# Second attention: maxima issued in pairs, work moved off VectorE beside the projections, stack loads moved to SyncE

## The reference

```python
def _L1_attn_ref(x, attn_qkvw, attn_qkvb, attn_ow, attn_ob):
    HEADS = 32
    B, S, H = x.shape                      # 1, 1024, 512
    hd = H // HEADS                        # 16
    scale = 1.0 / np.sqrt(hd)
    qkv = x @ attn_qkvw + attn_qkvb
    qkv = qkv.reshape(B, S, 3, HEADS, hd)
    q, k, v = (jnp.transpose(qkv[:, :, n], (0, 2, 1, 3)) for n in range(3))   # shortened
    scores = jnp.einsum('bhqd,bhkd->bhqk', q, k) * scale
    probs = jax.nn.softmax(scores, axis=-1)
    ctx = jnp.einsum('bhqk,bhkd->bhqd', probs, v)
    ctx = jnp.transpose(ctx, (0, 2, 1, 3)).reshape(B, S, H)
    return ctx @ attn_ow + attn_ob
```

## Time and profile before

| | |
|---|---|
| runs | 1622.28, 1622.95, 1625.58 us |
| the profiled execution, own time | 1626.14 us |
| its span, first to last instruction | 1624.2 us |
| mean granted TensorE clock | 0.961 |
| busy: PE, DVE, ACT, POOL | 1502.8, 1038.6, 810.8, 232.0 us |
| maxima on PE (line 1578), 512 | 187.1 us busy |
| their reductions on DVE (line 1681), 512 | 319.7 us busy |
| scores (line 1595), 256 | 158.1 us busy |
| mix (line 1610), 1024 instructions | 139.0 us busy |

### The profile page before, as it was taken

One profiled execution on the slowest core, in us unless ns is written; L12 is line 12 of the kernel. 1 busy time (PEld: TensorE's weight loads), 2 busy tenths in 40 slices (PEclk: granted clock), 3 DMA queues, 4 the chain that ended last, 5 costly groups with the idle time before them and its releaser, 6 DMA issues. The chain is left out here.

```text
span 1624.2 us, 22378 instructions
## 1 busy us (share of the span) xinstructions
PE 1502.8 (93%) x8030; PEld 991.4 (61%) x8030; DVE 1038.6 (64%) x2048; ACT 810.8 (50%) x1467; POOL 232.0 (14%) x233
## 2 busy tenths in 40 slices
PE   6867999999999999959979999898999999999987
PEld 4645776666777676647868887786553333333264
DVE  5744666666666666644643433564888999999245
ACT  5325666666666666641221221222117777777834
POOL 2762111112111111100000000001000122331200
PEclk9977999999999999989979999998989999999999
DMA  4142221212122221134212110117420222320001
GB/s 137 53 191 72 85 69 63 69 63 69 63 92 76 69 69 40 34 103 162 97 53 77 59 59 20 52 50 186 148 27 14 72 74 76 77 66 15 18 14 46
DMA packets 63298, 116.83 MB, mean 72 GB/s; under 512 B 12830, under 2 KB 32414, under 8 KB 61902
## 3 DMA queue, kind: packets, MB, share of 16 engines
q1 hardware_dynamic: 59956, 106.63, 20.6%
q10 hardware_dynamic: 3168, 8.65, 2.1%
q0 software_dynamic: 64, 0.11, 0.0%
HBM read 83.04 MB, written 29.66 MB: 69 GB/s over the span
## 5 line engine op out<-in xcount | busy, mean ns | idle before, releaser
L1681 DVE TENSOR_REDUCE ah_minus_half<-ah_ring 128x1 f32<-128x512 f32 x512 | 319.7, 679 | 40.3 <-PE ah_ring L1578 40.0
L968 DVE CUSTOM_DVE_ANT_0 mh_score<-mh_score,mh_mask 128x128 f32<-128x128 f32 (+7 forms) x256 | 195.8, 765 | 179.4 <-PE mh_score L781 179.3
L1641 ACT ACTIVATE ah_probs<-ah_score 128x1024 f32<-128x1024 f32 x256 | 248.7, 1023 | 114.6 <-PE ah_score L1595 113.6
L890 ACT ACTIVATE mh_probs<-mh_score,mh_minus_max 128x128 f32<-128x128 f32 (+7 forms) x256 | 189.6, 741 | 39.8 <-DVE mh_minus_max L968 35.8
L1578 PE MATMUL ah_ring<-ah_k_stack,ah_q_stack 48*128 48x512 f32 x512 | 187.1, 468 | 14.1 <-DVE ah_minus_half L1681 4.2
L1578 PEld LDWEIGHTS ah_ring<-ah_k_stack,ah_q_stack 48*128 48x128 f32 x512 | 82.8, 190 | 176.9 <-DVE ah_minus_half L1681 161.5
L1595 PE MATMUL ah_score<-ah_q_stack,ah_k_stack 49*128 49x512 f32 x512 | 158.1, 445 | 3.8 <-DVE ah_v L1705 2.3
L779 PE MATMUL mh_score<-shared,h_hi 128*128 128x512 f32 (+3 forms) x384 | 152.2, 396 | 3.0 <-ACT mh_probs L890 2.9
L1041 POOL TENSOR_TENSOR h_lo<-mh_pe,h_hi 64x512 fp32r<-64x512 f32 x64 | 81.9, 1279 | 459.0 <-ACT h_hi L876 455.4
L1610 PE MATMUL ah_mix<-ah_probs,ah_v 128*32 128x512 f32 x1024 | 139.0, 615 | 0.6 <-ACT ah_probs L1641 0.6
L781 PE MATMUL mh_score<-shared,h_lo 128*128 128x512 f32 (+3 forms) x384 | 133.0, 346 | 0.0
(11 more groups left out here) (222 smaller groups left out, 2854.7 us busy)
## 6 DMA issues: line engine op xcount, KB each, us to landing
mh_w<-in_w_pairs SPq DMA_DIRECT2D x16, 896.0 KB, 5.6
x<-in_w_inner SPq DMA_DIRECT2D x14, 768.0 KB, 4.1
pe_scratch<-fr_pe_out SPq DMA_DIRECT2D x4, 2048.0 KB, 6.6
mh_pe<-pe_scratch SPq DMA_DIRECT2D x16, 512.0 KB, 4.0
mh_spread<-inverse_scratch SPq DMA_DIRECT2D x64, 128.0 KB, 2.9
a_scratch<-mh_mixed SPq DMA_DIRECT2D x32, 256.0 KB, 2.4
x<-a_scratch SPq DMA_DIRECT2D x8, 1024.0 KB, 6.9
qk_scratch<-ai_ring SPq DMA_DIRECT2D x32, 256.0 KB, 2.7
```

The source lines that it names most:

```text
L890: nc.scalar.activation(probs[:, s % 2, 0:width], score_ps[s % 2][:, base:base + width], ACT.Exp, bias=minus_max[:, s % 4:s % 4 + 1], scale ...
L968: nc.vector.tensor_tensor_reduce(out=scores, in0=scores, in1=mask[:, S - width:S], scale=-1.0, scalar=3e38, op0=ALU.add, op1=ALU.min, accu ...
L1641: nc.scalar.activation(probs[:, 2 * (u % 2) + c, :], score_ps[c][:].rearrange("p e n -> p (e n)"), ACT.Exp, scale=MHA_SCALE).then_inc(prob ...
L1681: nc.vector.reduce_max(minus_half[:, m:m + 1], ring[:, m % 3, :], AX.X, negate=True).then_inc(max_taken, 1)
```

## The change

1. Maxima go in pairs. `two_maxima` waits once, for reduction m-2 (m is the first of the pair), and issues m and m+1, one on each row half.
2. Beside products 8 to 23 there are 6 maxima for each (FIRST = 96), a pair after step 0, a pair after steps 1 and 2, a pair after step 3. The other 416 are spread over the first 116 units, 4 or 2 for each: a pair ahead of c0 and a pair ahead of c1, none ahead of the mix (AHEAD 4 for 6; the inversions keep 6 as INVERTED).
3. DVE keeps only the first four lower parts and weight pieces 0 and 1. From product 4 on ACT evicts each bank twice (once rounded, once whole into a new tile `full`), and POOL subtracts. POOL splits weight pieces 2 to 11. Pieces 6 and 7 come at product 5 instead of 7.
4. ACT copies V without a bias; POOL adds the bias of V after the division.
5. SP holds back the stores of products 4 and later until the stacks of group 0 have landed.
6. The reloads of stacks for groups 3 to 7, one transfer behind each unit's exponentials on ACT before, are issued by SP in one run of twelve.
7. `as_c` and `as_spread` share memory with `full`; the bias comes as one small tensor.

```diff
     def product(self, pe, n, steps):
         if steps[0] == 0:
-            wait(pe, self.lo_ready, min(n - 3, self.NQK))
+            wait(pe, self.first_lo_ready, min(n - 3, 4))
+            wait(pe, self.full_ready, min(n - 7, self.NQK - 4))
             wait(pe, self.v_ready, n - 3 - self.NQK)
...
     def take_upper(self, act, n):
...
+        if n >= 4:
+            wait(act, self.lo_ready, n - 7)
+            self.nc.scalar.activation(self.full[:, n % 4, :], self.bank(n), ACT.Identity, bias=self.bias[:, row:row + 1]
+                                      ).then_inc(self.full_ready, 1)
...
+    def take_lower(self, pool, n):
+        pool.wait_ge(self.hi_ready, n + 1)
+        pool.wait_ge(self.full_ready, n - 3)
+        self.nc.gpsimd.tensor_tensor(self.ring[:, n % 4, 1, :], self.full[:, n % 4, :], self.ring[:, n % 4, 0, :].bitcast(F32),
+                                     ALU.subtract).then_inc(self.lo_ready, 1)
...
     def divide(self, pool, g, half):
...
+        self.nc.gpsimd.tensor_scalar(self.c[rows, cols], self.c[rows, cols], self.bias[rows, 2 * ND + k:2 * ND + k + 1], None, ALU.add
+                                     ).then_inc(self.multiplied, 1)
...
-        FIRST = 5 * (products.COUNT - FROM)
-        AHEAD = 6
+        FIRST = 6 * (products.COUNT - FROM)
+        AHEAD, INVERTED = 4, 6
...
-            return min(FIRST - (-unit * (TOTAL - FIRST) // (UNITS - NT - AHEAD)), TOTAL)
+            return min(FIRST - 2 * (-unit * (TOTAL - FIRST) // (2 * (UNITS - NT - AHEAD))), TOTAL)
...
-            now, then = maxima_at(n), maxima_at(n + 1)
-            return (now, min(now + (then - now + 1) // 2, then), min(now + (3 * (then - now) + 2) // 4, then))[stage]
+            return maxima_at(n) if stage == 0 else min(maxima_at(n) + 2, maxima_at(n + 1))
...
+            def reload_stacks(g, row_halves):
+                wait(sp, scores_ready, 2 * NUNIT * (g - DEPTH + 1))
+                load_stacks(sp, g, row_halves)
...
             load_stacks(sp, 0, (0,))
+            sp.wait_ge(stacks_in[0], 16 * (STACK_DMAS + 2))
             for n in range(4, products.NQK):
...
                 shares.put(sp, g - 1, 1, out, out_taken)
+                if DEPTH <= g + 2 < GROUPS:
+                    reload_stacks(g + 2, range(2))
                 put_max(g, 1)
...
-            def one_maximum(m):
-                wait(pe, max_taken, m - 2)
-                maximum(m).then_inc(max_ready, 1)
+            def two_maxima(m):
+                wait(pe, max_taken, m - 1)
+                for n in range(2):
+                    maximum(m + n).then_inc(max_ready, 1)
...
-                for part in range(2):
-                    products.product(pe, n, range(2 * part, 2 * part + 2))
+                for part, steps in enumerate(((0,), (1, 2), (3,))):
+                    products.product(pe, n, steps)
...
+            for t in range(NT):
+                act.wait_ge(products.ready, products.NQK + t + 1)
+                nc.scalar.copy(v[t][:].rearrange("p (h r) -> p h r", h=H)[:, :, 0:HD],
+                               products.bank(products.NQK + t).rearrange("p (h r) -> p h r", h=H)).then_inc(products.v_ready, 1)
```

More of the change, by code:

```diff
@@ L1313, in take_upper @@
         if n == 0:
[L1314 removed]
+            act.wait_ge(self.bias_in, 16)
         act.wait_ge(self.ready, n + 1)
@@ L1318, in take_upper, with take_first_lower @@
         row = kind * ND + blk
-        self.nc.scalar.activation(self.ring[:, n % 4, 0, :], self.bank(n), ACT.Identity, bias=self.bias_qk[:, row:row + 1]
+        self.nc.scalar.activation(self.ring[:, n % 4, 0, :], self.bank(n), ACT.Identity, bias=self.bias[:, row:row + 1]
                                   ).then_inc(self.hi_ready, 1)
-    def take_lower(self, dve, n):
+        if n >= 4:
+            wait(act, self.lo_ready, n - 7)
+            self.nc.scalar.activation(self.full[:, n % 4, :], self.bank(n), ACT.Identity, bias=self.bias[:, row:row + 1]
+                                      ).then_inc(self.full_ready, 1)
+    def take_first_lower(self, dve, n):
         kind, blk, _ = self.place(n)
@@ L1325, in take_lower @@
         dve.wait_ge(self.hi_ready, n + 1)
-        self.nc.vector.scalar_tensor_tensor(self.ring[:, n % 4, 1, :], self.bank(n), self.bias_qk[:, row:row + 1],
-                                            self.ring[:, n % 4, 0, :].bitcast(F32), ALU.add, ALU.subtract).then_inc(self.lo_ready, 1)
+        self.nc.vector.scalar_tensor_tensor(self.ring[:, n % 4, 1, :], self.bank(n), self.bias[:, row:row + 1],
+                                            self.ring[:, n % 4, 0, :].bitcast(F32), ALU.add, ALU.subtract).then_inc(self.first_lo_ready, 1)
+    def take_lower(self, pool, n):
[3 more added lines that the diff above has]
+                                     ALU.subtract).then_inc(self.lo_ready, 1)
+        pool.wait_ge(self.lo_ready, n - 3)
     def store(self, sp, n, qk):
@@ L1331, in store @@
         first = (kind * ND + blk) * P
-        for part, done in ((0, self.hi_ready), (1, self.lo_ready)):
-            sp.wait_ge(done, n + 1)
+        for part in range(2):
+            if part == 0:
+                sp.wait_ge(self.hi_ready, n + 1)
+            elif n < 4:
+                sp.wait_ge(self.first_lo_ready, n + 1)
+            else:
+                sp.wait_ge(self.lo_ready, n - 3)
             sp.dma_start(qk[part, first:first + P, half * BANK:(half + 1) * BANK],
@@ L1539, in then @@
                 pool.wait_ge(pool_done, n[0])
+            for job in range(products.NQK):
+                if job >= 4:
+                    products.take_lower(pool, job)
+                for i in pieces.get(job, ()):
+                    products.lower(pool, i)
+                    pool.wait_ge(products.w_ready, i + 1)
             for t in range(NT):
@@ L1623, in _ @@
                     while done < maxima_before(n, stage):
-                        one_maximum(done)
-                        done += 1
+                        two_maxima(done)
+                        done += 2
                     if n < UNITS and stage < 2:
@@ L1700, in turn @@
                 last.then_inc(rows_ready, 1)
-            def take_value(n):
-                t = n - products.NQK
-                dve.wait_ge(products.ready, n + 1)
-                nc.vector.tensor_tensor(v[t][:].rearrange("p (h r) -> p h r", h=H)[:, :, 0:HD],
-                                        products.bank(n).rearrange("p (h r) -> p h r", h=H),
-                                        products.bias_v[:].rearrange("p (h r) -> p h r", h=H), ALU.add).then_inc(products.v_ready, 1)
             for half in range(NHALF):
                 nc.vector.memset(minus_max[half][:], 0.0).then_inc(cleared, 1)
-            pieces = {1: (2, 3), 3: (4, 5), 7: (6, 7), 8: (8,), 9: (9,), 10: (10,), 11: (11,)}
             m, joined, turned, inverted = 0, 0, 0, 0
             for n in range(products.COUNT + 1):
-                if n < products.NQK:
-                    products.take_lower(dve, n)
-                elif n < products.COUNT:
-                    take_value(n)
-                for i in pieces.get(n, ()):
-                    products.lower(dve, i)
-                until = maxima_beside(n + 1, 1) if n + 1 < products.COUNT else FIRST if n < products.COUNT else TOTAL
+                if n < 4:
+                    products.take_first_lower(dve, n)
+                until = maxima_beside(n + 1, 2) if n + 1 < products.COUNT else FIRST if n < products.COUNT else TOTAL
                 while m < until:
@@ L1971, in two_layers @@
                 stage = layer.enter_context(ExitStack())
+                offsets["full"] = nc.sbuf_base
+                full = sb("full", [P, 4, BANK])
                 products = Products(nc, layer, stage, io, h, at, d_free)
@@ L1989, in two_layers @@
                          "zeros": at("ah_zeros", [P, D], F32, "down_lo", 6 * S), "scales": at("ah_scales", [P, D], F32, "down_lo", 6 * S + D)}
-                shares = Shares(nc, layer, scratch, h)
+                shares = Shares(nc, layer, scratch, h, products.bias, at, "full")
                 mha_heads(nc, io, scratch, later, shares, products, place)
```

52 lines of the change are left out of this document (20 added, 32 removed).

## The result

The changed kernel takes 1634.16 us, the median of five runs (1633.22 to 1642.62), against 1624.22 for the kernel before beside it (1622.28 to 1626.34). The ratio of the runs is 1.0078, 95% interval 1.0048 to 1.0107: slower by 0.5 to 1.1%. The profiled execution took 1633.22 us, its span is 1631.3 us, 7.1 more than before, and its mean granted clock 0.969 instead of 0.961. It is the shortest of the five runs; by the medians the change costs 9.9 us, by the ratio 12.7.

The account below looks back on a forecast made before the run. Units were taken as bound by a loop of latencies over three PSUM banks, not one engine. Units +10.5, products +5.3, step -6.1 gave +9.7 on the profiled 1626.14 us: 1635.8, less 3.2 for the median, 1632.7 (1622 to 1643).

Parts of the forecast that it names:

- The pair in the units: Second attention's units: long ones 2.94 us instead of 2.70, short 1.89 instead of 2.12, fewer last units; +10.5 us.
- The 4 us for DVE's side work: Units 5 to 115: DVE's turns, joins and inversions add 4 us to the loops instead of 9.7.
- Products: V products: three groups of maxima instead of two make a product 4.67 us instead of 4.39; +5.3 us, ends 0 and +8.
- The first stacks: Stack loads before the first maximum: held stores were not in their way, so the hold costs 0, ends -3 and +3.
- the two signs named: First maximum: still near 1129.6 us as forecast; near 1126 would mean the stores had been in the way.
- Step to the units: Last V product to unit 5: scores start sooner, full clock from 1207 on, 13.9 us instead of 19.95; -6.1 us.
- the 1.3 us for the table load: Step to the units: ACT's load of the exponential's table, hidden before, now stands ahead of the first exponential.
- Off the path: ACT's evictions, POOL's work, SP's reloads and the maxima's shorter lead have room; no term in the sum.
- DVE as the pace: Rival, faster: pairs relieve PE and DVE sets the units' pace; 1580 us, 4%.
- hidden changes of tile: Rival, faster: tile changes hide beside the V products, about 3.8 us each; 1619.5 us, 6%.
- a hardly longer unit: Rival: c1 streams beside the second pair, long units 2.83 us instead of 2.94; 1623 us, no change, 9%.
- The slow clock in the first units: Rival, slower: four long units at about 4.8 us, step term +1 instead of -6.1; 1640 us, 17%.

Follow-up runs that it names:

- Experiment 4: Kernel before with only the units' maxima in pairs ahead of c0 and c1, 80 maxima beside the products as before: 1650.11 us, ratio 1.0159.
- experiment 1: Changed kernel with the second pair of a unit ahead of the mix instead of ahead of c1: 1621.22 us, ratio 0.9981 against the kernel before.
- experiment 9: Kernel of experiment 1 with SP's twelve stack reloads issued behind the row transfers (put_max) instead of ahead: 1619.73 us, ratio 0.9977 against the kernel before.
- the two pairs that share their runs: Hold on the stores added to the kernel before, ratio 0.9993; and taken out of the kernel of experiment 9, 1620.48 against 1619.73 us.
- experiment 3: Changed kernel without SP's hold on the stores of product 4 and later: 1640.18 us, ratio 1.0098 against the kernel before.
- experiment 6: Changed kernel with one unused exponential on ACT ahead of its copies of V, to load the table early: 1636.93 us, ratio 1.0077 against the kernel before.
- experiment 2: Changed kernel with single maxima in the units, 4 or 3 each, pairs kept beside the products: 1625.09 us, ratio 1.0003 against the kernel before.
- experiment 12: Changed kernel with single maxima in the units and SP's reloads behind the row transfers: 1616.78 us, ratio 0.9955 against the kernel before.
- experiments 7: Changed kernel with maxima beside the products in two groups of three instead of three pairs: 1635.36 us, ratio 1.0066 against the kernel before.
- experiment 5: Kernel of experiment 1 with stack reloads on ACT again, two behind the exponentials of each of six units: 1619.92 us, ratio 0.9974 against the kernel before.
- 11: Kernel of experiment 9 without SP's hold on the stores of product 4 and later: 1620.48 us, ratio 0.9978 against the kernel before.

## Why the prediction was right

Predicted 1632.7 us (1622 to 1643), measured 1634.16: slower, by nearly the size forecast. That it came so close is in part luck. Between the profiled executions +7.1 us was measured for the +9.7 of the sum: the products cost 2.2 us less than forecast, the step to the units gave back 1.5 less, the units cost 0.3 less, and 1.7 us fell in stages that the sum had at 0 (the first two and the rest). The prediction then took 3.2 us off for the median, which now lies 0.9 above the profiled execution. And two of the five runs took 1640.51 and 1642.62 us, at the top of the range; no profile shows why.

**The pair in the units: right.** Long unit 2.94 and short unit 1.89, both as worked out, the stretch 305.1 for 305.2, the last units -4.2 for -4.0. DVE idles 0.37 us ahead of a long unit, where about half a microsecond was forecast. Experiment 4 gives the loss by itself, and experiment 1 shows the step it rests on: only what stands behind the wait for the first reduction is on the path. The 4 us for DVE's side work were right too (3.7); with c1 out of the way 7.9 us stand over the loops (experiment 9).

**Products: the pitch right, the term too big.** 4.67 was forecast and 4.68 measured. The last maxima were through 75.6 us after the first one against 72.5 before: +3.1 instead of +5.3. The term took the slow stretch over from before, 10.2 us of half clock, and the profile had 3.4. In other profiles it lasted 6.8 to 17.1.

**The first stacks: not refuted.** Costed at 0; the two pairs that share their runs show some 1 us, not clear of 0. The first maximum came at 1127.14, between the two signs named (1129.6 and 1126), 0.9 of it from an earlier start of the loads. In the changed kernel itself only experiment 3 tests it, against another set of runs.

**Step to the units: smaller than forecast.** 15.4 us from the last product's maxima to unit 5 for 13.9, so -4.6 instead of -6.1. The clock was not full from 1207 on: 3.4 us of half clock lay over the first mix (1.86 us to the next pair instead of 1.00). And the 1.3 us for the table load in the sum were wrong: experiment 6 shows them hidden. Units 0 and 1 took 5.9 us and not 4.6; the half clock over the mix is 0.9 of the 1.3 more, and the second pair waits for DVE twice (0.54 and 0.39 us).

**Off the path: nearly right.** POOL's addition was costed at under 1.3 us and took 1.56, beside hundreds of idle us (POOL, columns: busy, mean ns, idle before):

```profile
L1411 POOL TENSOR_SCALAR as_c<-as_c,ai_bias 64x512 f32<-64x512 f32 x15 | 23.5, 1563 | 1.5
```

The reloads ahead of `put_max` cost the changed kernel nothing that shows (0.3 us of waits for the rows); its long units hid them. They became a cost as the units got shorter: 1.4 us in the stretch between experiments 1 and 9, nothing clear in the totals, and 8 us in the totals between 2 and 12. Of the 15.4 us between the profiled stretches of these two, 3.7 are waits for the rows; the stretch of experiment 2 also held 23.9 us of half clock, which by my estimate (half of its length) is nearly all of the rest.

**The rivals.** DVE as the pace, hidden changes of tile and a hardly longer unit are excluded by the rows above. The slow clock in the first units came for 3.4 us in the profiled execution, not for four units; in near relatives of the kernel it came for 10.2 and 13.7 us (experiments 7 and 2), so that it stayed short here is not shown to be a property of the change.

## What to carry to other kernels

Two instructions joined to share a slot also share the later of their waits, and everything between that wait and the loop's next start is on the path: work out the loop (here 1.28 + what stands behind the wait + the mix), not the busy shares, and put independent work ahead of the waiting pair. Small transfers that an engine will wait for are issued ahead of bulk ones on the queue, and a check of that is due again once the loop beside them gets shorter. A difference of a few us between single profiles, or between medians from different sets of runs, is not the worth of an edit: take pairs that share their runs.

## What the runs showed of the hardware

- A transfer of 8 KB (`as_sums`) issued by SP, 4 us behind one of 256 KB, took 18 us to land while twelve transfers of 128 KB were issued on ACT's queue (experiment 5); with the same bulk issued behind it on SP, and the same 256 KB ahead, it was there within 15.3 us and no engine waited for it (experiment 9).
- After a wait of PE the granted clock fell to 0.50 for 3.4 to 17.1 us, in the same place of near-identical programs: 3.4 us behind the first scores in experiment 9, 17.1 in 11, whose only edit lies 80 us earlier. Within the units experiment 2 had it behind waits of 0.83 and 1.74 us, 10.2 us each; experiment 12 had none behind waits of 0.83 and 0.81, experiment 1 none behind one of 1.13.
- From the issue of the same twelve loads to the first maximum it took 10.2 to 12.9 us from run to run.
